# Building the head stacks with selection matmuls, two heads to a stack, in place of DMAs (one decoder layer, one core)

## Time and profile before

| | |
|---|---|
| median of 3 runs | 259.3 us (259.08 to 259.61) |
| the profiled execution | 258.73 us, its span in the trace 256.9 us |
| granted TensorE clock, mean | 0.861 of 2.4 GHz |
| busy, share of the span | PE 76%, DVE 67%, ACT 36%, POOL 23% |
| DMA | 9125 packets, 9.41 MB |

### The profile page before, as it was taken

The page is one execution under the profiler, slowest core; times in us unless marked ns, Lnnn a source line. Parts: engine busy times, 40 slices in busy tenths (PEclk is TensorE's granted clock), DMA queues, the critical chain, the costliest instruction groups (busy, mean ns, idle before and its releaser), DMA issues.

```text
span 256.9 us, 3649 instructions
## 1 busy us (share of the span) xinstructions
PE 195.1 (76%) x1272; PEld 89.9 (35%) x1280; DVE 172.0 (67%) x423; ACT 91.6 (36%) x138; POOL 58.0 (23%) x85
## 2 busy tenths in 40 slices
PE   3617609988750843788599989999999979999951
PEld 2401103322340531544243435665554322232321
DVE  4719998864560896298988988874317766567742
ACT  4600006578300010343183856568652221222210
POOL 6299995002450176000000000010000100001111
PEclk9955557999995795699999999999999985899975
DMA  6961894000266459620202000000000000000000
GB/s 152 183 71 16 101 104 47 4 2 0 32 55 59 43 73 117 81 87 3 84 0 86 0 1 4 3 2 6 0 3 0 0 4 0 0 0 11 10 0 20
DMA packets 9125, 9.41 MB, mean 37 GB/s; under 512 B 1492, under 2 KB 7052, under 8 KB 9108
## 3 DMA queue, kind: packets, MB, share of 16 engines
q1 hardware_dynamic: 7668, 6.82, 16.3%
q0 software_dynamic: 1440, 2.37, 8.4%
HBM read 4.02 MB, written 0.26 MB: 17 GB/s over the span
## 4 chain that ended last, share of the span: by engine, by line
PE 54%; DVE 19%; DMA 16%; SPq 4%; issue 3%; ACT 2%; POOL 0%; POOLq 0%; another core or an unknown queue 0%; ACTq 0%; DVEq 0%
PE y L528 12%; DVE mneg L695 12%; PE w L601 7%; PE t L601 7%; DMA q_stack_A<-mrow 4%; DMA k_stack_b<-part_k 4%; SPq L378 4%; PE t L497 4%; PE w L452 3%; DMA q_stack_A<-part_q 3%; DMA q_stack_B<-mrow 3%; PE t L479 2%; PE t L486 2%; PE t L602 2%; PE w L602 2%
## 5 line engine op out<-in xcount | busy, mean ns | idle before, releaser
L695 DVE TENSOR_REDUCE mneg<-w 128x1 f32<-128x512 f32 (+2 forms) x128 | 78.1, 651 | 29.3 <-PE w L450 10.0
L887 ACT ACTIVATE probs<-t 128x1024 f32<-128x1024 f32 x48 | 48.4, 1023 | 52.9 <-PE t L479 30.7
L1000 POOL TENSOR_SCALAR rstd<-mv 128x2 f32<-128x2 f32 (+1 forms) x8 | 1.8, 225 | 169.2 <-DVE mv L645 169.2
L452 PE MATMUL w<-k_stack_c,q_stack_A 128*128 128x512 bf16 x56 | 21.2, 390 | 4.6 <-DVE mneg L695 4.0
L442 PE MATMUL w<-k_stack_a,q_stack_A 128*128 128x256 bf16 x64 | 16.1, 360 | 9.6 <-DMA q_stack_A<-part_q 6.8
L884 ACT ACTIVATE probs<-t 128x768 f32<-128x768 f32 x16 | 12.8, 811 | 21.4 <-PE t L491 21.4
L497 PE MATMUL t<-q_stack_A,k_stack_c 128*128 128x256 bf16 x128 | 19.3, 273 | 1.0 <-DVE mneg L695 0.4
L601 PE MATMUL w<-w1T,xT 128*128 128x512 f32 x32 | 19.6, 698 | 0.0
L601 PE MATMUL t<-w1T,xT 128*128 128x512 f32 x32 | 19.5, 694 | 0.0
L528 PE MATMUL y<-probs,v_c 128*32 128x256 f32 x256 | 19.0, 389 | 0.4 <-issue 0.2
L445 PE MATMUL w<-k_stack_b,q_stack_B 128*128 128x128 bf16 x32 | 7.7, 239 | 11.2 <-DMA k_stack_b<-part_k 7.8
(11 more groups left out here) (168 smaller groups left out, 334.3 us busy)
## 6 DMA issues: line engine op xcount, KB each, us to landing
w1T<-in_w1T SPq DMA_DIRECT2D x8, 256.0 KB, 3.1
k_stack_c<-y_sb POOLq DMA_DIRECT2D x6, 256.0 KB, 11.7
rest<-in_rest SPq DMA_DIRECT2D x1, 772.0 KB, 9.7
q_stack_A<-part_q SPq DMA_DIRECT2D x12, 64.0 KB
q_stack_B<-part_q SPq DMA_DIRECT2D x12, 64.0 KB
bias_row<-in_rows SPq DMA_DIRECT2D x1, 384.0 KB, 6.3
k_stack_b<-part_k POOLq DMA_DIRECT2D x6, 64.0 KB, 6.4
k_stack_b<-part_k SPq DMA_DIRECT2D x6, 64.0 KB
```

What stands on the lines that cost most here:

```text
L452: last = nc.tensor.matmul(o[:], q[:, head, q0 + qt * P:q0 + (qt + 1) * P], k_stack_c[:, head, b * TC:(b + 1) * TC], start=True, stop=True)
L695: emptied(V.tensor_reduce(out=dst, in_=src, axis=AX.X, op=ALU.max, negate=True), s)
L887: ins = A.activation(dst, o[:], ACT.Exp)
```

## The change

- A stack now has 64 rows, and two heads (an even one and the next) lie above each other in 128 partitions: `q_stack` for A, B and C (C has its own now), `k_stack_b`, `k_stack_c` are [128, 8 pairs, tokens]. A row block of 48 holds the six terms, rows 48 to 50 of each half the maximum. S and U contract over 64 partitions, the lower or the upper half. In U the two halves alternate and write to different halves of their PSUM region.
- The weights keep the heads in their natural order, so that a head's 8 channels lie together, and a group of 32 partitions holds 4 heads. `sel` [128, 2, 2, 3, 128] holds 0/1 matrices that DVE makes at the start (28 small copies, L762). The new step RS multiplies them with the bf16 parts: 12 matmuls of 256 columns for four pairs of q or k of part B (and q of A and C), 12 of them of 512 columns for two tiles of k of part C (6 each), 3 for k of A; each is 32 rows deep (L433). The result in PSUM is exact, and ACT (L1016, L1014) or DVE (L826, k of B) copies it as bf16 into the stack, adding the ones where k has them. There are 4 RS for q of A, 2 for k of A, 4 each for qB, kB, qC and 8 for kC.
- The step PA (projection of sequence 1 for part A) and KC (k of C) are now steps of the plan instead of the head of the program.
- The cut of q and k into parts is done by ACT (first part, straight from PSUM) and DVE; for k of B it was POOL. The cut of k of C stays on POOL; the one of the expert bias goes to POOL.
- The causal mask, 128 x 128 in one matmul before, takes two of 64 columns (`at_q`, `tri_q`; `at_k`, `tri_k`).
- The maximum rows are sent by two DMAs (L1159) instead of one. The stack DMAs and the big fills are gone.
- `bias_sel` and `b1_stack` of the expert bias have 128 rows instead of 24, the rest zero.
- PV of part C starts with two units of `probs` instead of all.

```diff
-TERMS = ((0, 0, 0), (8, 1, 0), (16, 2, 0), (32, 0, 1), (40, 1, 1), (96, 0, 2))
+TERMS = ((0, 0), (0, 1), (1, 0), (1, 1), (2, 0), (0, 2))
...
+    first = [("RS", "qA", 0, 0), ("RS", "kA", 0), ("RS", "qA", 0, 1)]
+    second = [("PA", 1), ("RS", "qA", 1, 0), ("RS", "kA", 1), ("RS", "qA", 1, 1)]
+    context = [("KC",), ("VC", 0), ("VC", 1)] + [("RS", "kC", b, g, j) for b in range(B) for g in range(2) for j in range(2)]
...
-        if k == "S" and s[1] != "A":
-            return [(("PROJ", s[2]), STACK)]
+        if k == "S":
+            p, b, g = s[1:4]
...
+            return [(("RS", "qC", b, g), 0.1)] + [(("RS", "kC", b, g, j), 0.1) for j in range(2)]
...
+            def select(o, cols, side, j, r, group, values):
+
+                rows = slice(32 * group, 32 * group + 32)
+                return nc.tensor.matmul(o[:, cols], sel[rows, side, j, r, :], values[rows, :], start=(r == 0), stop=(r == 2))
...
-                        last = nc.tensor.matmul(o[:], q[:, head, q0 + qt * P:q0 + (qt + 1) * P],
-                                                k_stack_c[:, head, b * TC:(b + 1) * TC], start=True, stop=True)
+                        last = nc.tensor.matmul(o[:], q[:, q0 + qt * P:q0 + (qt + 1) * P],
+                                                k_stack_c[half, pair, b * TC:(b + 1) * TC], start=True, stop=True)
...
+                elif kind == "RS":
+                    _, name, b = s[:3]
+                    side = 0 if name[0] == "q" else 1
+                    pe.wait_ge(s_parts["kC" if name == "kC" else f"{name}{b}"], 3)
...
+                        for j in range(2):
+                            for r in range(3):
+                                for i in range(2):
+                                    c0 = i * 512 + j * T
+                                    last = select(o, slice(c0, c0 + T), side, j, r, 2 * g + i,
+                                                  parts_of[name][:, r, b * T:(b + 1) * T])
...
-                        for kt in range(4):
-                            k0 = b * TC + kt * P
-                            last = nc.tensor.matmul(o[:, kt * T:(kt + 1) * T], k_stack_c[:, head, k0:k0 + P],
-                                                    q[:, head, q0:q0 + T], start=True, stop=True)
+                        pair = 4 * g + 2 * hh + j % 2
+                        for n in range(2):
+                            for i in range(2):
+                                half = rows_of(i)
+                                c0 = i * 512 + n * T
+                                k0 = b * TC + (2 * (j // 2) + n) * P
+                                last = nc.tensor.matmul(o[:, c0:c0 + T], k_stack_c[half, pair, k0:k0 + P],
+                                                        q_stack[part][half, pair, q0:q0 + T], start=True, stop=True)
...
+                elif kind == "RS" and EVICT[s[1]] == "act":
+                    o = restacked(s, wait_full(act, s))
+                    if s[1][0] == "k":
+                        act.wait_ge(s_rows, 1)
+                        emptied(A.activation(stacked(s), o, ACT.Identity, bias=row_ones[:, 2:3]), s)
+                    else:
+                        emptied(A.activation(stacked(s), o, ACT.Copy), s)
...
-        bias_sel = sb("bias_sel", [3 * E, E, P], BF16)
+        bias_sel = sb("bias_sel", [P, E, P], BF16)
...
-                    sp.dma_start(q_stack[part][MROW:MROW + 3, 8 * g:8 * g + 8, b * T:(b + 1) * T],
-                                 mrow[:, mb % NROW, :]).then_inc(s_shift[mb], 16)
+                    for i in range(2):
+                        row = HALF * i + MROW
+                        sp.dma_start(q_stack[part][row:row + 3, 4 * g:4 * g + 4, b * T:(b + 1) * T],
+                                     mrow[12 * i:12 * i + 12, mb % NROW, :]).then_inc(s_shift[mb], 16)
```

More of the change, by code:

```diff
@@ L327, in build @@
         s_parts = {k: sem(f"parts_{k}") for k in (
[L328 to L330 removed]
+            "qA0", "kA0", "qA1", "kA1", "qB0", "kB0", "qC0", "qB1", "kB1", "qC1", "kC", "b1")}
+        s_b1 = sem("b1_stacked")
         s_mpart = sem("max_parts")
@@ L363, in words, with rows_of, stacked, restacked @@
             return t.bitcast(F32)
+        def rows_of(head):
+            return slice(HALF * (head % 2), HALF * (head % 2) + HALF)
+        def stacked(s):
+            _, name, b = s[:3]
+            if name == "kA":
+                return k_stack_a[:, b * T:(b + 1) * T]
+            if name == "kC":
+                g, j = s[3:]
+                return k_stack_c[:, 4 * g + j:4 * g + j + 3:2, b * TC:(b + 1) * TC]
+            dst = k_stack_b if name == "kB" else q_stack[name[1]]
+            return dst[:, 4 * s[3]:4 * s[3] + 4, b * T:(b + 1) * T]
+        def restacked(s, o):
+            if s[1] == "kA":
+                return o[:, 0:T]
+            return o[:].rearrange("p (n q) -> p n q", n=2 if s[1] == "kC" else 4)
         def head_values(v):
             return v[:, 0:H * VD].rearrange("p (h w) -> p h w", w=VD)[:, :, 0:D]
-        def stack_key(part, b):
-            return "kC" if part == "C" else f"k{part}{b}"
-        def make_stack(eng, dst, parts, side, key, which=range(3), done=None):
-            for part in which:
-                eng.wait_ge(s_parts[key], part + 1)
-                for term in TERMS:
-                    if term[1 + side] == part:
-                        eng.dma_start(dst(slice(term[0], term[0] + D)), parts[:, part, :]).then_inc(done or s_stack[key], 16)
         @block.tensor
@@ L477, in _ @@
                         for kt in range(2):
-                            rhs = q[:, 8 * g + j:8 * g + j + 5:4, q0:q0 + T]
-                            last = nc.tensor.matmul(o[:, kt * 512:(kt + 1) * 512],
-                                                    k_stack_a[:, q0 + kt * P:q0 + (kt + 1) * P], rhs,
-                                                    start=True, stop=True)
+                            for i in range(2):
+                                c0 = i * 512 + kt * T
+                                half = rows_of(i)
+                                last = nc.tensor.matmul(o[:, c0:c0 + T], k_stack_a[half, q0 + kt * P:q0 + (kt + 1) * P],
+                                                        q_stack[part][half, 4 * g + j, q0:q0 + T], start=True, stop=True)
@@ new lines, in _ @@
+                            nc.tensor.matmul(o[:, i * 512:i * 512 + T], k_stack_b[half, pair, q0:q0 + P],
+                                             q_stack[part][half, pair, q0:q0 + T], start=True, stop=False)
+                        for n in range(2):
+                            for i in range(2):
+                                half = rows_of(i)
+                                c0 = i * 512 + n * HALF
+                                nc.tensor.matmul(o[:, c0:c0 + HALF], at_k[half, n, :], tri_k[half, n * HALF:(n + 1) * HALF],
+                                                 start=False, stop=(n == 1))
@@ new lines, in _ @@
+            for side in range(2):
+                for j in range(2):
+                    heads = ident_32[:, 16 * j:16 * j + 16].rearrange("p (i d) -> p i d", d=D)
+                    for r, first_term, count, step in TERM_RUNS[side]:
+                        for i in range(2):
+                            dst = sel[:, side, j, r, HALF * i:HALF * i + 6 * D].rearrange("p (t d) -> p t d", d=D)
+                            ins = V.tensor_copy(dst[:, first_term:first_term + step * (count - 1) + 1:step, :],
+                                                heads[:, i:i + 1, :].to_broadcast([P, count, D]))
@@ L660, in _ @@
+            ins.then_inc(s_sel, 1)
+            for i in range(2):
+                ins = V.tensor_reduce(out=row_ones[:, i:i + 1], in_=ident[:, HALF * i + MROW:HALF * i + MROW + 3],
+                                      axis=AX.X, op=ALU.max)
+            link(ins)
+            V.tensor_tensor(row_ones[:, 2:3], row_ones[:, 0:1], row_ones[:, 1:2], ALU.add).then_inc(s_rows, 1)
             dve.wait_ge(ld_first, 16)
             V.tensor_scalar(bias_col[:, 0:3], bias_col[:, 0:3], SCALE, None, ALU.mult).then_inc(s_bias, 1)
-            for b in range(B):
-                cols = slice(b * T, (b + 1) * T)
+            dve.wait_ge(s_bias, 1)
```

518 lines of the change are left out of this document (280 added, 238 removed), and 2 rows, old and new, of the table COSTS.

## The result

The changed kernel takes 286.05 us (median of four, 284.59 to 288.53) against 259.19 in the same sitting: ratio 1.1076, with a 95% interval of 1.099 to 1.116. It is slower, by 10 us more than the 276 forecast, inside the range. The profiled execution took 288.53 us, its span 286.8; it is the slowest of the four. Where the executions of a kernel fall apart, ratios here use the faster ones, medians all of them.

The account below looks back on a forecast made before the run. DMA waits (27.1 us) and what follows bound the kernel to 104, then DVE's reductions to 172, then PE. Last TY at 221.5 plus 53.2 gives 274.7, span 17.8 over 256.9; 258.7 + 17.8 gives 276 us, range 257 to 288.

Parts of the forecast that it names:

- First scores, first U: Start of part A: first scores at 11.5 instead of 17.6, first U at 31.5 instead of 37.9.
- `sel` late: Rival at the start: DVE's 28 copies wait for POOL's mask operations, first scores 6 us later, 282 us; chance 0.12.
- First TY: End of part A, sequence 0: PV, VC0 and two U in a row, TY at 51 instead of 56.4.
- Stacks of part B: PROJ of sequence 0 to first scores of part B: 9.5 us against 17.7, scores at 69.7; first U at 80.8.
- The term for which the change is made: First scores of part B: 12 DMA issues and the 10.99 us landing leave the path, gain 13.6 us.
- the walk: The prediction's step-by-step timing of the new order, milestone to milestone on the trace's time axis, ending at 274.7.
- Here the lead goes: Before part C: 27.4 us of steps in line, about 12 of DVE work; scores at 108.2, gain left 1 us.
- The second stretch: Part C, copied maxima at 121.2 to TY at 150.6; reductions of sequence 1 only at 157, loss 25 us.
- Last reduction to end: Last reduction at 199.2, last TY 22.3 us later at 221.5, end 53.2 us after that, F at 1.10.
- The order keeps its lead: Fast rival: pauses before part C and between its sequences shrink to 19 and 17 us, 257 us; chance 0.20.
- Rows in turns: Rival on RS: two row groups do not overlap, 0.65 us on each of some 14 RS, 285 us; chance 0.12.
- The change does not do what it says: Rival: wider bias does not shorten F, or maximum rows still take 8 us or more, 283 us; chance 0.08.

Follow-up runs that it names:

- kc_early: Changed kernel with planner urgency of the selection matmuls for k of part C at 1.0 instead of -0.5: 263.2 us, ratio 1.011 to the kernel before.
- own_order_full_rows: Changed kernel, own order, S and U of part C over all 128 rows (sums of two heads' scores): 285.5 us, ratio 1.104.
- own_order_full_bc: Changed kernel, own order, S and U of parts B and C over 128 rows, causal masks still on 64: 304.1 us, ratio 1.183.
- context_early: Changed kernel with planner urgencies raised for RS of k of part C (1.0) and its v projection (0.9): 254.8 us, ratio 0.980.
- full_rows: context_early with S and U of part C over all 128 rows, each tile the sum of two heads' scores: 248.9 us, ratio 0.960.
- the best version: On context_early with RS urgency 1.0 and PA cost edit: q of part C zero-padded per head, S and U on 128 rows: 246.8 us, ratio 0.951.
- bias_rows: Kernel before with only the expert bias stored on 128 rows instead of 24, rest zero: 251.5 us, ratio 0.973.
- rs_twice: context_early with every selection matmul issued twice into the same place: 259.7 us.

## Why the prediction was right or wrong

- *First scores, first U.* Right, 10.2 for 11.5 and 32.2 for 31.5. The 28 copies took 2.33 us, 0.08 from one to the next where 0.15 was taken (and the 2.1 to 6.3 of the working should have been 2.8 to 6.2); the rival "`sel` late" did not happen, though POOL made masks beside them. RS of part A went at 0.107 a matmul, as in single file at the full clock or side by side at the half one; it was the second (below).
- *First TY, +4.5 us over the forecast.* The step that failed took durations of PV and U from rows of the full clock. PV of part A took 1060 ns instead of 592. One PV of the second pair in the changed kernel (50.4 and 52.8), and one of the same pair in `kc_early` (49.1 and 50.4), which has the same order up to there:

```profile
50.40 1.93 PE L614 MATMUL y<-probs,v_a 128*32 128x512 f32 x8
...
55.52 1.09 PE L628 MATMUL t<-ident,y_sb 128*128 128x128 f32 x8 [0.99 <-ACT probs L997]
```
```profile
50.40 1.06 PE L614 MATMUL y<-probs,v_a 128*32 128x512 f32 x8
...
53.10 1.09 PE L628 MATMUL t<-ident,y_sb 128*128 128x128 f32 x8 [0.96 <-ACT probs L997]
```

  `kc_early` came to the full clock (2.4 GHz) ahead of this PV, the changed kernel behind it, and 2.4 of the 4.5 us lie between their two TY. The two other kernels with this order, `own_order_full_rows` and `own_order_full_bc`, have their TY at 53.2 as well: this part belongs to the profiled execution, not to the change.
- *Stacks of part B.* From PROJ to the first scores it took 10.3 us, forecast 9.5. The term for which the change is made was right: 9.2 us of lead at the first scores, 15.7 at the first U. Between the two it took 14.5 us, forecast 11.1: the walk counted 16 reductions and two MS, but a PV and a TY of part A, sequence 1, stand between these tiles (at 79.4 and 85.1, 1.94 and 1.97 us, at a clock of 0.50), and DVE waited for them and, 0.34 us a time, for the next pair of tiles. The maximum rows themselves are fast now, as walked: 2.8 us from the copy to the one U that waits for them (153.1 to 155.9), 3.6 taken.
- *"Here the lead goes".* Right in kind, and the point of the document: `context_early` changes nothing but the order and takes 31 us away. The pause was costlier than walked: 33.4 us instead of 27.4 from the first U of part B to the first scores of part C. The clock was at 0.64 there from 97 to 122; TY took 1.94 instead of 1.09 us, VC 2.07 instead of some 1.1, the RS of q of part C 3.00 for two instead of 1.66, those of k 2.74 instead of 1.47, and two steps of PV, 1.51 each, 3.02 instead of 1.72. That sums to 5.7 of the 6.0 us, an estimate, since it takes all of them to lie on the path. The second stretch, from the copied maxima to TY of part C, took 32.3 us (135.0 to 167.3), walked as 29.4. Here the clock of S and U is not the reason: `own_order_full_rows`, with 0.93 for 0.50 from 138 to 150, took 31.6. The walk missed tenths at many places, 3.3 us for 2 to the first reduction among them.
- *Last reduction to end.* 71.8 us, forecast 75.5: last TY 20.9 behind it (22.3), and 50.9 from there (53.2). F at 1.07 for 1.10 right; alone in the kernel before it was worth 5.8, in `full_rows` 8.6. The terms listed ahead of the last TY come to 24.4 with 4 U at 0.61, not to the 22.3 written; 20.9 were measured.
- *The rivals.* "The order keeps its lead", 257, did not happen in the change, but its place was right: `context_early`, with scores of part C from 91.0 on, takes 254.8. "Rows in turns" fell. "The change does not do what it says" fell in both halves.
- *The size, 286 for 276.* In the profiled execution, the slowest of the four, the span is 12.1 us over the forecast. Along the milestones 4.5 us were missed up to the first TY, 3.4 between scores and U of part B, 6.0 in the first pause, 3.7 from the copied maxima to the reductions of sequence 1; 5.4 were given back behind them. What the first three have in common is the lower clock, which no step of the walk had: I read it as a property of the kernel before, where it was 1.00 in part C. That the sum came so near is in part luck, steps taken too long against steps taken too short.
- *What was not shown.* That the 6 us missed in the first pause are the clock's rests on durations in traces; `own_order_full_rows` could not raise it there, and `own_order_full_bc` brought drains with it.

## What to carry to other kernels

When a change takes transfers off the front, walk the order behind it to the engine that bounds the middle, and look for steps that now come in one row with nothing for that engine between them: here two numbers of a planner were worth 31 us, more than the waits removed. Halving the rows of a matmul was not free on TensorE even where the columns stayed: part C ran at 0.66 with half rows and at 0.93 with whole ones, and everything between its matmuls slowed down with it. Keep neighbouring matmuls on one row count; each change cost 0.11 to 0.15 us. And measure what a small part of a change does alone: the wide bias is about half of what the best version gains.

## What the runs showed of the hardware that was not expected

- Busy PE and high clock are two things: at 64 rows PE was busy 35 of 38 us at 0.50 (1.2 GHz); at 128 rows, with holes, 0.93 to 1.00. Nor is it rows alone: 0.50 also with PE busy 18 of 18 us, scores on 128 rows and masks on 64 (`own_order_full_bc`), and 13 of 16 us, mostly scores on 128 rows (`own_order_full_rows`); and 0.86 with half rows and twice the RS (`rs_twice`).
- The row of the granted clock can't be trusted at the start of a trace. In the changed kernel it shows 1.00 up to 72, yet a pass of PV of part A takes 1060 ns up to 52 and 592 from 52.8 on, and a matmul of 64 rows and 256 columns 417 and later 266. So the mean clock of an execution says little by itself: `bias_rows` has 0.92 and 0.85 with 251.9 and 250.6 us. From 18 to 38 the kernel before shows 0.50 in one trace and, in `bias_rows`, 1.00 for the same matmuls with the same length (median 417 and 407 ns, against 273 at the full clock). The durations tell; and so do the early scores, which are bound by DVE and hide it.
- By the durations the kernel before was at the full clock from 42.5 on, the changed one only from 52.8.
